# A two-layer block with paged attention: the passage to attention re-ordered by need, first projections begun by parts, new values stored by one transfer per tile

## What is computed

```python
q, k, v = x @ Wq.T, x @ Wk.T, x @ Wv.T            # 32 query heads, 8 key/value heads of 128
q, k = rope(rmsnorm(q, qw), pos), rope(rmsnorm(k, kw), pos)
k_all = concat(k_cache[block_table], k)            # 16 pages of 32 tokens, then 32 new ones
v_all = concat(v_cache[block_table], v)
probs = softmax(mask(q @ k_all.T / sqrt(128)))
a = (probs @ v_all) @ Wo.T
x = x + conv(a, s4_kernel(Lambda, p, q, Vc, Ct, Bp, step)) + D * a
z = x @ W.T + b + lora(x, ids)
x = x + z @ Wf.T + bf + gated_lora_experts(z)
```

## Time and profile before

| | |
|---|---|
| Time, median of 3 runs | 1321.12 us (1319.19 to 1321.59) |
| The profiled execution | 1318.64 us, its span 1316.9 us |
| Busy share: TensorE, VectorE, ScalarE, POOL | 95%, 62%, 62%, 58% |
| Mean granted TensorE clock | 0.982 |
| HBM read, written | 203.33 MB, 10.49 MB |

### The profile page before, as it was taken

How to read it: one execution, slowest core, us unless ns; L and a number is a source line. 1 busy time by engine, 2 the same in 40 slices (tenths; PEclk the granted TensorE clock), 3 DMA queues, 4 the chain that set the end, 5 groups by cost and what they waited for, 6 DMA issues and landing times.

```text
span 1316.9 us, 28777 instructions
## 1 busy us (share of the span) xinstructions
PE 1247.0 (95%) x7378; PEld 1040.4 (79%) x7378; DVE 810.3 (62%) x1724; ACT 810.3 (62%) x2256; POOL 767.4 (58%) x901
## 2 busy tenths in 40 slices
PE   6899969999999997998989999699999999999998
PEld 4678859998989985774757788599998989978856
DVE  5976647676776766772146866377676776755422
ACT  3676558788888873332135766478788888744330
POOL 3443448888888874543033434388888888854330
PEclk9999979999999998999989999899999999999999
DMA  7241388888888835305134321888888888333300
GB/s 244 88 137 64 111 233 229 233 239 240 233 234 234 235 78 179 134 0 190 35 110 133 113 96 64 247 227 228 238 243 241 234 236 231 112 107 134 96 33 33
DMA packets 148202, 214.84 MB, mean 163 GB/s; under 512 B 25940, under 2 KB 120470, under 8 KB 142102
## 3 DMA queue, kind: packets, MB, share of 16 engines
q1 hardware_dynamic: 128742, 202.75, 52.5%
q10 hardware_dynamic: 18576, 9.05, 2.5%
q0 software_dynamic: 800, 2.10, 0.5%
HBM read 203.33 MB, written 10.49 MB: 162 GB/s over the span
## 4 chain that ended last, share of the span: by engine, by line
PE 81%; DVE 6%; issue 3%; DMA 3%; ACT 3%; ACTq 2%; POOL 0%; SPq 0%; DVEq 0%; POOLq 0%
PE PS L1032 17%; PE PS L1000 9%; PE PS L931 4%; PE PS L927 4%; PE PS L923 4%; PE PS L1041 4%; PE PS L1092 3%; PE PS L1083 3%; PE PS L1089 3%; PE PS L967 2%; PE PS L1134 2%; PE PS L969 2%; PE PS L902 2%; PE PS L985 2%; PE PS L989 2%
## 5 line engine op out<-in xcount | busy, mean ns | idle before, releaser
L574 POOL TENSOR_TENSOR kv_parts<-kv,k_hi 128x544 fp32r<-128x544 f32 x192 | 258.7, 1348 | 41.6 <-ACT k_hi L765 40.0
L1032 PE MATMUL PS<-probT,kv 128*128 128x128 f32 x2048 | 270.4, 275 | 0.0
L527 POOL TENSOR_TENSOR ring_parts<-ring,kv_parts 128x512 fp32r<-128x512 f32 x96 | 128.0, 1341 | 227.4 <-ACT kv_parts L641 227.4
L1032 PEld LDWEIGHTS PS<-probT,kv 128*128 128x128 f32 x2048 | 248.8, 192 | 0.1
L1492 DVE COPY probT<-PS 128x512 f32<-128x512 f32 x256 | 175.5, 686 | 3.1 <-PE PS L1000 3.1
L804 ACT ACTIVATE ring<-ring,smin 128x544 f32<-128x544 f32 x192 | 143.8, 749 | 38.3 <-DVE smin L1486 37.2
L1486 DVE CUSTOM_DVE_ANT_0 ring<-PS,mask,rq 128x544 f32<-128x544 f32 x192 | 150.0, 781 | 21.9 <-PE PS L990 13.8
L765 ACT ACTIVATE k_hi<-kv 128x544 fp32r<-128x544 f32 x192 | 125.9, 657 | 52.4 <-PE PS L990 48.8
L605 POOL TENSOR_TENSOR ring_parts<-ring,kv_parts 128x512 fp32r<-128x512 f32 x64 | 89.1, 1397 | 105.8 <-ACT kv_parts L844 105.8
L562 POOL TENSOR_SCALAR ring<-ring,rinv 128x512 f32<-128x512 f32 x192 | 133.6, 696 | 0.0
L923 PE MATMUL PS<-kv_parts 128*128 128x512 f32 x384 | 115.0, 419 | 16.8 <-ACT kv_parts L641 14.2
(11 more groups left out here) (214 smaller groups left out, 2738.9 us busy)
## 6 DMA issues: line engine op xcount, KB each, us to landing
kv<-in_kpages SPq DMA_DIRECT2D x512, 128.0 KB, 2.3
kv<-in_vpages SPq DMA_DIRECT2D x496, 128.0 KB, 3.3
ring<-in_w SPq DMA_DIRECT2D x46, 1024.0 KB, 4.9
kv<-in_xT SPq DMA_DIRECT2D x4, 1024.0 KB, 8.8
v_new<-kv ACTq DMA_DIRECT2D x64, 64.0 KB, 2.5
k_new<-kv ACTq DMA_DIRECT2D x16, 256.0 KB, 2.3
kv<-k_new SPq DMA_DIRECT2D x32, 128.0 KB, 2.7
kv<-v_new SPq DMA_DIRECT2D x32, 128.0 KB, 2.4
```

The lines of the kernel that those rows point to most:

```text
L574: nc.gpsimd.tensor_tensor(kbuf_lo(par)[:, :, g, :], kbuf(par)[:, :, g, :], k_hi[:, e % 2, :].rearrange("p (j t) -> p j t", t=PSIZE), ALU.s ...
L1032: mm = nc.tensor.matmul(PS[:, at:at + D], vbuf(bpar)[:, c, gg * D:(gg + 1) * D], probT[:, g % 2, c * P:(c + 1) * P], start=(c == 0 and a = ...
```

## The change

It has four parts, none of which changes what is computed.

1. **Start by parts.** x and block 0 are loaded as four pairs of 256 KB (`load_first`). ScalarE's `upper_first`, VectorE's `lower_x` and POOL's `lower_of` split each part as it lands; TensorE multiplies block 0 part by part for all four tiles, in banks 4 to 7. For the second half all of that stands in the last stage of the first, between z and the qk products. Six of ScalarE's nine small loads go to SP, between the parts, and the first activation table is loaded by a dummy activation (`warm`).
2. **New values** are stored by one transfer for each tile (the row order in `v_new` is changed for it). Values of block 0 are staged in a place of their own, so those stores no longer wait for each other.
3. **SP's order at the passage.** Keys of sequence 0 come before blocks 12 and 13; its 16 value pages all come by SP, by fours as `turned` allows; then keys of sequence 1; both sequences' new values; values of sequence 1; block 15. Block 14 comes after attention. (Probabilities use slot 2 of the ring instead of slot 3.)
4. **TensorE, ScalarE, VectorE at the passage.** Block 11's first three tiles are each followed by two turns; scores of groups 0 and 1 come before the fourth tile. ScalarE copies q and splits keys of groups 0 and 1 first, loads Exp's table by a dummy, then mixes stores of values with q copies.

The core of the diff:

```diff
+            def load_first(h):
+
+                if h:
+                    sp.wait_ge(w_free, h * (BLOCKS // 2) + 1)
+                for c in range(KC):
+                    rows = slice(c * P, (c + 1) * P)
+                    sp.dma_start(xA[:, c, :], xT_d[rows, h * HT:(h + 1) * HT]).then_inc(x_in[c], 16)
+                    sp.dma_start(slot(0)[:, c, :], w_d[0, :, c * 512:(c + 1) * 512]).then_inc(w_first_in[c], 16)
+                    if not h and c == 1:
+                        for r in range(4):
+                            sp.dma_start(lens_i[32 * r:32 * r + 32, :],
+                                         bass.AP(lens_td.tensor, r * HALVES * TILES,
+                                                 [[0, 32], [1, HALVES * TILES]])).then_inc(misc_in, 16)
+                        sp.dma_start(dls[:, :], bass.AP(dls_d.tensor, 0, [[0, P], [1, 2]])).then_inc(misc_in, 16)
+                        sp.dma_start(bias[:, :], bias_d).then_inc(misc_in, 16)
+
+            load_first(0)
...
+                sp.wait_ge(table_in, 16 * h + 32)
+                for n in range(2):
+                    sp.wait_ge(kn_out[n], 8 * KU * (h + 1))
+                    sp.wait_ge(vn_out[n], h * (8 * KU) + 32)
+                sp.sem_inc(sp_past, 1)
+                pages = page_registers(0)
+                load_keys(0, 0, pages)
+                load_w(h, 12)
+                load_w(h, 13)
+                for j in range(NPP):
+                    if j % 4 == 0:
+
+                        sp.wait_ge(turned, NQK * (h + 1) - 6 + 2 * (j // 4))
                         sp.sem_inc(sp_past, 1)
...
+                    load_value_page(0, j, pages[j])
+                sp.wait_ge(proj_ready, PROJ * (h + 1))
                 sp.sem_inc(sp_past, 1)
-                load_kv(0, 0, True)
-                load_kv(1, 1, True)
+                pages = page_registers(1)
+                load_keys(1, 1, pages)
+                for n in range(2):
+                    sp.wait_ge(vn_out[n], 8 * KU * (h + 1))
+                load_new_values(0, 0, first_vnew_in)
+                load_new_values(1, 1, v_in[1])
+                for j in range(NPP):
+                    load_value_page(1, j, pages[j])
+                load_w(h, 15)
...
-                load_w(h, 15)
+                load_w(h, 14)
...
-                    load_x(1)
-                    for n in range(3):
+                    load_first(1)
+                    for n in range(1, 3):
...
+            def upper_first(h):
+
+                for c in range(KC):
+                    act.wait_ge(x_in[c], 16 * (h + 1))
+                    nc.scalar.activation(x_hi[:, c, :], xA[:, c, :], ACT.Copy).then_inc(xhi_ready, 1)
+                    act.wait_ge(w_first_in[c], 16 * (h + 1))
+                    nc.scalar.activation(block_hi[:, c, :], slot(0)[:, c, :], ACT.Copy).then_inc(bhi_ready, 1)
+
+            upper_first(0)
...
-                    for n in range(4):
-                        act.dma_start(vn_d[ds(h * HB + 4 * m + n, 1), :, col * D:(col + 1) * D]
-                                      .rearrange("o (a t) d -> t (o a) d", a=GU),
-                                      stage[n * SEQ:(n + 1) * SEQ, m % 2, :].rearrange("t (a d) -> t a d", a=GU))\
-                            .then_inc(vn_out[m % 2], 16)
+                    act.dma_start(vn_d[ds(h * HB + 4 * m, 4), :, col * D:(col + 1) * D]
+                                  .rearrange("b (t a) d -> (b t) a d", a=GU),
+                                  v_stage(col, m).rearrange("p (a d) -> p a d", a=GU))\
+                        .then_inc(vn_out[m % 2], 16)
...
-                act.wait_ge(row_ready, 16 * (h + 1))
-                act.sem_inc(act_past, 1)
-                mask_of(0, 0)
-                act.wait_ge(turn_read, NQK * (h + 1))
+                act.wait_ge(turn_read, h * NQK + NQK - LAG)
                 upper_q(0, 0)
                 upper_keys(0, 0, 0)
                 upper_keys(0, 0, 1)
-                for g in range(HK):
+                root(2, qstat[1], qstat[0])
+                nc.scalar.activation(warm[:, 2:3], ident[:, 0:1], ACT.Exp)
+                for m in range(2):
+                    store_v(1, m)
+                    for n in range(2):
+                        keep_q(KU + 4 * TILES - LAG + 2 * m + n, 1)
+                act.wait_ge(row_ready, 16 * h + 4)
+                act.sem_inc(act_past, 1)
+                mask_of(0, 0)
+                store_v(1, 2)
+                for n in range(2):
+                    keep_q(KU + 4 * TILES - 2 + n, 1)
+                act.wait_ge(turn_read, NQK * (h + 1))
+                step(0, 0, 0, True)
+                store_v(1, 3)
+                act.wait_ge(row_ready, 16 * (h + 1))
+                act.sem_inc(act_past, 1)
+                for g in range(1, HK):
...
+                with act.If(h < 1):
+                    upper_first(1)
...
-                pe.wait_ge(out_ready, KC * (h + 1))
-                whole_block(0)
+                for c in range(KC):
+
+                    pe.wait_ge(xhi_ready, h * KC + c + 1)
+                    pe.wait_ge(bhi_ready, h * PROJ + c + 1)
+                    for m in range(TILES):
+                        nc.tensor.matmul(bank(4 + m), x_hi[:, c, m * P:(m + 1) * P], block_hi[:, c, :],
+                                         start=(c == 0), stop=False)
+                    pe.wait_ge(xlo_ready, h * KC + c + 1)
+                    for m in range(TILES):
+                        nc.tensor.matmul(bank(4 + m), x_lo[:, c, m * P:(m + 1) * P], block_hi[:, c, :],
+                                         start=False, stop=False)
+                    pe.wait_ge(blo_ready, h * PROJ + c + 1)
+                    for m in range(TILES):
+                        mm = nc.tensor.matmul(bank(4 + m), x_hi[:, c, m * P:(m + 1) * P], slot_lo(0)[:, c, :],
+                                              start=False, stop=(c == KC - 1))
+                        if c == KC - 1:
+                            mm.then_inc(proj_ready, 1)
...
-                whole_block(11, after=NQK - LAG)
-                turn(NQK - 2)
-                turn(NQK - 1)
-
-
-                pe.wait_ge(v_read, 2 * TILES * (h + 1))
-                pe.wait_ge(turn_read, NQK * (h + 1))
+                for m in range(3):
+
+                    if m < 2:
+                        pe.wait_ge(swp_ready, h * NQK + (NQK - TILES) + m + 1)
+                    else:
+                        pe.wait_ge(rot_ready, NQK * (h + 1))
+                    tile(11, m, bank(m if m < 2 else 6))
+                    turn(NQK - LAG + 2 * m)
+                    turn(NQK - LAG + 2 * m + 1)
...
+                scores(0, 0, 0, True)
+                scores(0, 0, 1, True)
+                pe.wait_ge(rot_ready, NQK * (h + 1))
+                tile(11, 3, bank(7))
+                attend(0, 0, True, 2)
```

261 lines of the change are left out of this document (121 added, 140 removed).

## The result

The changed kernel takes **1305.38 us** (median of 4 runs, 1301.47 to 1306.34) where the kernel before, measured beside it, takes 1321.36: ratio 0.9876, 95% interval 0.9861 to 0.9891. It is faster by 16 us, 1.2%, where 30 were forecast, and the time lies above the forecast's range of 1281 to 1302. The profiled run of after took 1306.34 us with a span of 1304.4; that of before had 1316.9.

A forecast was written before the change was run, and what follows sets the result against it. TensorE was taken as the bound, busy 1247.0 of 1316.9 us, with gaps at starts and passages. Terms 7.7 + 7.6 + 8.9 + 6.1 = 30.3 us gave 1288.3 for the profiled run, 1291 for the median; range 1281 to 1302.

The forecast's parts named there:

- start of the first half: From the first loads to the first rotation: it comes at 28.4 instead of 36.20; 7.7 us, bounds 4 and 8.8.
- three signs named for being wrong: Last part landing after 14 us, a one-transfer store taking over 1 us to issue, or k_hi waiting in several tiles.
- passages, TensorE's side: From block 11's start (T) to first use of new values (the mark): 11.2 us earlier, second half about 9.9.
- handed back by the queue's side: Attention after each passage: tile 2's late keys leave 7.6 us of 11.2, and 6.1 of 9.9 in the second half.
- start of the second half: Block 0's splitting moves into the first half's tail; first rotation at 691.6 instead of 700.46: 8.9 us, bounds 7 and 10.
- TensorE's block 0 ends at 16 to 18: First half's start: TensorE finishes block 0 at 16 to 18 us and block 1 at about 30, so it follows.
- ScalarE's row: First half's start: four one-transfer stores begin at 18, each 0.6 copy, 0.38 issue, 0.15 waits, and end at 22.5 us.
- The angles: VectorE at the first start: begun at about 12.7, 2.5 us quicker with POOL idle, ready at about 22.7 instead of 29.1.
- 0.9 us of issue, and its data: SP's stream after the passage: two stores' rereads and block 15 before tile 2's keys cost 0.9 us issue, plus data time.
- Block 15's 3 us: Its 1 MB load ahead of tile 2's keys delays them by 3 us, bounds 0 and 4.9.
- Rival 2: In attention the key stream limits for longer: five tiles give 1296 us, all tiles 1306, taken 1298; chance 0.14.
- Rival 3: At the first start the 256 KB parts travel slowly and the start gains nothing: 1298.5 us; chance 0.07.

The follow-up runs named there:

- e3: Changed kernel with SP's six small loads moved behind the last part of x and block 0: 1306.22 us, ratio 0.9884 to the kernel before.
- e4: Changed kernel with only the last part of block 0 multiplied tile by tile: 1301.79 us, ratio 0.9848 to the kernel before.
- e11: Changed kernel with x and block 0 loaded whole and block 0 multiplied tile after tile: 1306.73 us, ratio 0.9873 to the kernel before.
- e6: Changed kernel with new values, rows still exchanged, read by four transfers of 32 rows: 1315.02 us, ratio 0.9953 to the kernel before.
- e8: Changed kernel with plain read, four-transfer stores (first column's by SP), block 15 after attention, last part of block 0 tile by tile: 1301.1 us.
- e7: Kernel before with only the read of new values taking rows in exchanged order: 1327.35 us, ratio 1.0047 to the kernel before.
- e13: Changed kernel with POOL starting block 2's differences only after the rope tables: 1304.13 us, ratio 0.9869 to the kernel before.
- e2: Changed kernel with new values read back plainly, rows then in wrong order: 1294.51 us, ratio 0.979 to the kernel before.
- e1: Changed kernel with block 15 loaded after attention, behind block 14: 1301.69 us, ratio 0.9845 to the kernel before.
- e10: Changed kernel with both the plain read of new values and block 15 loaded after attention: 1295.46 us, ratio 0.9792 to the kernel before.

## Why the prediction was wrong

**The direction held, the sum did not**: 30.3 forecast, 12.5 between the traces (16 between the medians). Two terms failed: the start of the first half and, above all, what the queue takes back in the passages. None of the three signs named for being wrong appeared: the last part landed at 13.6, a store took 0.66 us at most to issue, and k_hi waited in tile 2 alone. They did not cover what failed.

| term | forecast | between the traces |
|---|---|---|
| start of the first half | 7.7 | 2.2 |
| passages, TensorE's side | 11.2 and 9.9 | 10.4 and 9.1 |
| handed back by the queue's side | 3.6 and 3.8 | 6.6 and 9.0 |
| start of the second half | 8.9 | 8.0 |
| rest of attention, handed back | none | 0.8 and 0.9 |

**Start of the first half, 7.7: mis-sized, 2.2.** Four steps failed. (1) "TensorE's block 0 ends at 16 to 18": I counted from the last part's landing; 48 multiplications, the first part's at half rate, took from 7.2 to 20.8. The last part landed at 13.6, not at 11.5 to 11.9, but e3 showed that this was not the limit. (2) ScalarE's row: a store took 1.45 us, not 1.13, since its issue takes 0.55 to 0.66 and not the 0.38 of the store of keys; and the stores, which I let begin at 18, begin at 20.1, because all tiles of block 0 end together. e4 shows it. (3) The angles were to end at 22.7, by 2.5 us saved with POOL idle. POOL was idle for only 1.4 us before its 6.5 us of block 1, the angles took 12.4 us as before, and ended at 26.0, level with the stores. (4) The comparison itself: the profiled run of before, which I took as its start, is a lucky one. In ten of the thirteen traces up to e11 the last two of eight rope tables take 1.5 us each, in three 0.42 (before, e6, e8). Like with like, the start won 38.9 (e7) less 34.0, or 36.2 less 31.6 (e13): 4.6 to 4.9 us.

What decides between the two is not shown. In either case POOL's difference begins while the sixth table runs, 0.06 to 0.09 us after that table's start, and the other two tables begin behind it. POOL's row is 2.16 us where they are quick (before, first line) and 1.51 where they are slow (after, second line): one of the two engines waits, now this one, now that.

```profile
35.16 2.16 POOL L527 TENSOR_TENSOR ring_parts<-ring,kv_parts 128x512 fp32r<-128x512 f32 x1 [12.27 <-ACT kv_parts L641]
...
30.77 1.51 POOL L565 TENSOR_TENSOR ring_parts<-ring,kv_parts 128x512 fp32r<-128x512 f32 x1 [7.12 <-ACT kv_parts L671]
```

**TensorE's side of the passage, 11.2 and 9.9: nearly right**, 10.1 from T in the first half, 9.1 from the first rotation in the second. Projections ended at T + 17.4 (18.1 forecast), but by two errors of opposite sign: the two groups' scores took 1.6 us in place of 3.0, and a wait for ScalarE's q copies 1.7 in place of 1.3. The mark came at T + 33.8 in place of 32.6.

**The queue's side, 3.6 and 3.8 handed back: the failed step.** It was 6.6 and 9.0, of which 0.8 each is VectorE's copy (above); in the second half all of the passage's gain went. "0.9 us of issue, and its data" priced block 15 and the number of the rereads but not their pattern, and the forecast asked only when tile 2's keys must be there. The runs showed that value pages of tile 1 came late first, 2.4 and 3.0 us of TensorE's wait. The read with exchanged rows was a line of the diff that I passed over: its 128 packets were counted like any 128 KB. e2 puts it at 10.9 us, e7 at 6.4 even where the stream had lead. With the plain read (e2) the hand-back is 3.0 and 2.7 us, block 15 included, close to what was forecast. Block 15's 3 us, the term I argued most about, is real beside the exchanged read (2.7 and 3.3 us of tile 2's step in e1) and 1.0 to 1.4 us without it (e10 against e2).

**Start of the second half, 8.9: right**, 8.0. By e11, whole loads and tile after tile would have given 3.7 more.

**Rivals.** Rival 2 (1298, "the key stream limits for longer") was the nearest in kind, for another reason than its own. Rival 3 leaned on the rule of the Trainium skill for 1 MiB or more per transfer ("DMA: Bandwidth & Descriptors", section "Rules for kernel authors"). The last part did land later than a whole load, 13.6 against 11.5 (12.5 with the small loads behind, e3), by 2.1 us and not by the 6 estimated; the first was there at 6.5, and the parts, multiplied as they came, still won 4.0 us at the first start. At the second start the data lay ready, and there parts cost 3.7 by the order of multiplying.
